# Two cross-attention blocks on one core: GpSimd instead of ScalarE normalises one head in four of the second block

## What is computed

```python
x = layer_norm(hidden_states, ln1_w, ln1_b)
q = (x @ q_w + q_b).reshape(B, LQ, H, HD).transpose(0, 2, 1, 3)
k = (encoder_hidden_states @ k_w + k_b).reshape(B, LK, H, HD).transpose(0, 2, 1, 3)
v = (encoder_hidden_states @ v_w + v_b).reshape(B, LK, H, HD).transpose(0, 2, 1, 3)
scores = jnp.einsum('bhqd,bhkd->bhqk', q, k) * scale
scores = jnp.where(mask, scores, mask_value)
attn = jax.nn.softmax(scores, axis=-1)
out = jnp.einsum('bhqk,bhkd->bhqd', attn, v)
hidden = out.transpose(0, 2, 1, 3).reshape(B, LQ, D) @ cproj_w + cproj_b + residual
```

## Time and profile before

| | us |
|---|---|
| median of three runs | 2257.14 |
| the profiled execution's own time | 2260.57 |
| its span, first to last instruction | 2258.8 |
| TensorE busy in the span | 2161.1 (96%) |
| VectorE busy | 1605.4 (71%) |
| ScalarE busy | 1183.9 (52%) |
| GpSimd busy | 943.8 (42%) |
| second block's attention, logits of step 0 to the last turns | about 1793 to 2090 |

### The profile page before, as it was taken

One profiled execution on the slowest core, in us unless ns is written; L12 is line 12 of the kernel. 1 busy time (PEld: TensorE's weight loads), 2 busy tenths in 40 slices (PEclk: granted clock), 3 DMA queues, 4 the chain that ended last, 5 costly groups with the idle time before them and its releaser, 6 DMA issues.

```text
span 2258.8 us, 36858 instructions
## 1 busy us (share of the span) xinstructions
PE 2161.1 (96%) x12468; PEld 2099.6 (93%) x12468; DVE 1605.4 (71%) x3635; ACT 1183.9 (52%) x2838; POOL 943.8 (42%) x898
## 2 busy tenths in 40 slices
PE   6999999999999999999999999999999899998899
PEld 5999999999999999999999999998899778887899
DVE  6777688777778877777887777777466487788353
ACT  4555465555555555555555555565243376667232
POOL 4314444241444424234342424432788332232597
PEclk9999999999999999999999999999999999998999
DMA  4646455554645555464555546454543667765243
GB/s 136 140 87 142 102 121 101 120 128 83 151 101 113 102 125 122 85 148 105 110 110 116 126 83 151 109 102 83 139 125 103 167 189 199 206 199 160 84 132 108
DMA packets 162454, 283.08 MB, mean 125 GB/s; under 512 B 35424, under 2 KB 92896, under 8 KB 162272
## 3 DMA queue, kind: packets, MB, share of 16 engines
q1 hardware_dynamic: 162272, 280.73, 52.5%
HBM read 237.66 MB, written 29.88 MB: 118 GB/s over the span
## 4 chain that ended last, share of the span: by engine, by line
PE 80%; DVE 6%; DMA 4%; ACT 3%; POOL 3%; issue 2%; SPq 2%; POOLq 0%; DVEq 0%; ACTq 0%
PE bank L838 76%; PE bank L926 3%; POOL mring L759 1%; DMA ctxN_raw<-in_ctx 1%; POOL mring L757 1%; DVE ln_c L1548 1%; DVE hT L1495 1%; SPq L636 1%; DVE lnb L1541 1%; PE bank L1106 1%; ACT prob L1340 1%; DMA k<-k_parts 1%; DVE prob L1662 1%; POOL ln_c L813 1%; DMA y_parts<-qs 0%
## 5 line engine op out<-in xcount | busy, mean ns | idle before, releaser
L838 PE MATMUL bank<-ctxT,kring 128*128 128x362 f32 x3456 | 629.6, 330 | 4.4 <-DVE qs L1495 2.7
L757 POOL TENSOR_SCALAR mring<-stage 128x512 fp32r<-128x512 f32 x325 | 233.3, 718 | 899.2 <-PE bank L838 734.2
L838 PEld LDWEIGHTS bank<-ctxT,kring 128*128 128x128 f32 x3456 | 587.2, 190 | 7.6 <-issue 4.7
L838 PE MATMUL bank<-pT,ctxN 128*128 128x400 f32 (+1 forms) x2304 | 470.0, 351 | 0.6 <-DVE U L1499 0.3
L759 POOL TENSOR_TENSOR mring<-stage,mring 128x512 fp32r<-128x512 f32 x325 | 444.9, 1369 | 27.1
L838 PEld LDWEIGHTS bank<-pT,ctxN 128*128 128x128 f32 (+1 forms) x2304 | 407.1, 188 | 2.4 <-issue 1.2
L838 PE MATMUL bank<-hT,mring 128*128 128x400 f32 x1608 | 320.0, 348 | 13.8 <-DVE hT L1495 10.5
L838 PEld LDWEIGHTS bank<-hT,mring 128*128 128x128 f32 x1608 | 296.1, 190 | 18.3 <-issue 15.0
L838 PE MATMUL bank<-U,mring 128*128 128x400 f32 x1536 | 303.3, 348 | 8.1 <-issue 6.3
L838 PEld LDWEIGHTS bank<-U,mring 128*128 128x128 f32 x1536 | 275.3, 188 | 10.3 <-issue 7.9
L1234 ACT ACTIVATE kT<-bank,cols 128x361 fp32r<-128x361 f32 (+1 forms) x288 | 160.8, 558 | 211.8 <-PE bank L838 211.7
(11 more groups left out here) (103 smaller groups left out, 2942.1 us busy)
## 6 DMA issues: line engine op xcount, KB each, us to landing
ctxT_raw<-in_ctx SPq DMA_DIRECT2D x72, 724.0 KB, 7.5
ctxN_raw<-in_ctx SPq DMA_DIRECT2D x256, 192.0 KB, 3.6
k<-k_parts SPq DMA_DIRECT2D x96, 181.0 KB, 3.7
stage<-in_wk SPq DMA_DIRECT2D x64, 256.0 KB, 4.1
stage<-in_wq SPq DMA_DIRECT2D x64, 256.0 KB, 4.5
stage<-in_wv SPq DMA_DIRECT2D x64, 256.0 KB, 4.0
stage<-in_wo SPq DMA_DIRECT2D x64, 256.0 KB, 2.7
stage<-in_fa SPq DMA_DIRECT2D x64, 256.0 KB, 2.6
```

Source lines behind the costliest of these rows:

```text
L757: nc.gpsimd.tensor_scalar(hi, src, 1.0, 1.0, ALU.mult, ALU.mult).then_inc(S.w_hi, 1)
L838: mm = pe.matmul(dst, parts_l[a], parts_r[b], start=first and k == 0, stop=last and k == len(order) - 1)
```

## The change

ScalarE's `normalise1` and its call are removed. GpSimd gets a `normalise1(s)` for head 4s+1: it waits for the reciprocal and multiplies the row in place with a TENSOR_SCALAR. The turn of this head waits for GpSimd's semaphore `p1_pool` instead of `p1_act`. In GpSimd's list the new entry is due at step s + 0.6 with priority 1. The context split of a batch element, one entry with both halves due at 2.2, becomes two entries, due 2.2 and 3.2.

```diff
-        S.p1_act = sem("p1_act")
+        S.p1_pool = sem("p1_pool")
...
-        def by_act(u):
+        def by_pool(u):
             return u % HG == 1
...
-            def split_context(i):
-
+            def second_context(n):
+
+                b, k = divmod(n, 2)
+                i = 4 * GN + b
                 pool.wait_ge(S.ctxT_in[i % 2], 16 * (i // 2 + 1))
-                for k in range(2):
-                    a = slice(k * HALF_T, (k + 1) * HALF_T)
-                    src, hi = ctxT_raw[:, i % 2, 1, a], ctxT[:, i % 2, 0, a]
-                    nc.gpsimd.tensor_scalar(hi, src, 1.0, 1.0, ALU.mult, ALU.mult).then_inc(S.cT_hi, 1)
-                    pool.wait_ge(S.cT_hi, 2 * i + k + 1)
-                    nc.gpsimd.tensor_tensor(ctxT[:, i % 2, 1, a], src, f32(hi), ALU.subtract).then_inc(S.cT_lo, 1)
-
-            def second_context(b):
-                split_context(4 * GN + b)
+                a = slice(k * HALF_T, (k + 1) * HALF_T)
+                src, hi = ctxT_raw[:, i % 2, 1, a], ctxT[:, i % 2, 0, a]
+                nc.gpsimd.tensor_scalar(hi, src, 1.0, 1.0, ALU.mult, ALU.mult).then_inc(S.cT_hi, 1)
+                pool.wait_ge(S.cT_hi, 2 * i + k + 1)
+                nc.gpsimd.tensor_tensor(ctxT[:, i % 2, 1, a], src, f32(hi), ALU.subtract).then_inc(S.cT_lo, 1)
+
+            def normalise1(s):
+                u = s * HG + 1
+                k = u % PB
+                pool.wait_ge(S.rden1_ready, u + 1)
+                x = prob1[0:LQ, k, 1:LT]
+                nc.gpsimd.tensor_scalar(x, x, rden[0:LQ, k:k + 1], 1.0, ALU.mult, ALU.mult).then_inc(S.p1_pool, 1)
...
-            extra += [(T_ATT1 + 4 * (b - 2) + 2.2, 2, second_context, b) for b in range(2, BATCH)]
+            extra += [(T_ATT1 + 4 * (b - 2) + 2.2 + k, 2, second_context, 2 * b + k)
+                      for b in range(2, BATCH) for k in range(2)]
+            extra += [(T_ATT1 + s + 0.6, 1, normalise1, s) for s in range(NS)]
...
             def turn1(u):
-                if by_act(u):
-                    pe.wait_ge(S.p1_act, u // HG + 1)
+                if by_pool(u):
+                    pe.wait_ge(S.p1_pool, u // HG + 1)
...
-            def normalise1(u):
-                act.wait_ge(S.rden1_ready, u + 1)
-                x, k = prob1[0:LQ, u % PB, 1:LT], u % PB
-                nc.scalar.activation(x, x, ACT.Identity, scale=rden[0:LQ, k:k + 1]).then_inc(S.p1_act, 1)
...
-                    if 0 <= u - 1 < NU1 and by_act(u - 1):
-                        normalise1(u - 1)
```

More of the change, by code:

```diff
@@ L1839, in _ @@
                         inverse1(u - 1)
-                    if 0 <= u - 1 < NU1 and not by_act(u - 1):
+                    if 0 <= u - 1 < NU1 and not by_pool(u - 1):
                         normalise1(u - 1)
```

## The result

The changed kernel took 2304.74 us as the median of four runs (2301.39 to 2307.31) against 2257.44 us for the kernel before (four runs, 2255.45 to 2263.1): ratio 1.021, 95% interval 1.0194 to 1.0226, 47.3 us slower. The forecast was 2313 us with 2288 to 2335. The profiled executions are 2303.11 and 2260.57 us, their spans 2301.3 and 2258.8, 42.5 us apart.

A forecast was written before the change was run, and what follows sets the result against it. Taken as bound by TensorE, busy 96%, its turns in fixed order. Stalls 60.6, given back -10.3, clock +7.9, ScalarE -2 make +56.2 us on the profiled 2260.57; carried over to the median 2257.14, 2313 us, range 2288 to 2335.

The forecast's parts named there:

- six named entries: GpSimd's queue: norm scale (steps 6, 27), tiles and context half (14), norm sum and tiles (20), squares' sum (23), tiles (30).
- The places: Steps 6, 14, 20, 23, 27, 30: GpSimd's release plus 0.55 us minus TensorE's turn, 60.6 us of stalls.
- The instruction: GpSimd's new 100x361 TENSOR_SCALAR, 32 times: 0.50 us each, bounds 0.49 to 0.89.
- The clock: TensorE at half clock after stalls, less two episodes that go with the key waits: +7.9 us, bounds 0 and +12.
- What is given back: Two key waits vanish and part of the last stall is hidden at the end: together -10.3 us.
- two key waits: TensorE's waits for keys, 2.85 and 4.50 us, behind SyncE's wait for the fourth tile's split, would go.
- The end: SyncE's store of step 31's head sums, ready earlier but held by the split: 2.9 us of the last stall hidden.
- port term: GpSimd's normalises and context halves beside VectorE's work at the shared port: 0, within 2 us; blocking rival +16 us, chance 0.07.
- ScalarE's relief: Copies queued behind ScalarE's normalise in the last steps come sooner: -2 us.
- ScalarE was to be 18.6 us less busy: Sign: removing 32 ScalarE instructions of 0.582 us lowers its busy time by 18.6 us.
- GpSimd's wait for the fourth tile of step 14: Sign: GpSimd's wait for fourth tiles, once 24.94 us before, stays as long as before.

The follow-up runs named there:

- the experiment with the earlier load: Changed kernel, but SyncE loads weight tiles by those due in step s instead of s - 1, GpSimd's order unchanged: 2279.07 us, ratio 1.0096.
- spread tiles and ScalarE normalising: Kernel before, ScalarE still normalising, weight tiles due one a step instead of four at once: 2251.42 us, ratio 0.9968.
- the halves together: Changed kernel with normalise due s - 0.1 (step 0 at 0.6), tiles one a step, both context halves in one entry: 2246.79 us, ratio 0.9958.
- earlier places and spread tiles: Changed kernel with normalise due s - 0.1 (step 0 at 0.6) and weight tiles one a step, context halves apart: 2243.01 us, ratio 0.9941.

## Why the prediction was right, point by point

The mechanism held: six stalls behind six named entries. The rise of the profiled execution was forecast as 56.2 us and measured as 42.5, 13.7 too much. That the median came nearer (2304.74 against 2313.3, 8.6 us) is luck: the profiled execution of before lay above its median and that of after below its own, which hides 5 us.

**The places.** The six steps were read off the sorted list, and the six stalls came at them. The only other wait of a turn over 2 us in the changed kernel is one of 2.48 us in step 29, for VectorE. Turn by turn the changed kernel lost 6.8, 15.3, 13.3, 5.2, 7.2 and 11.3 us more than the head before it (differences of the turns' starts between the two traces), 59.0 in all, forecast 7.0, 16.4, 13.2, 4.7, 7.6 and 11.7, 60.6. The release times of the trace of before could be used because what released GpSimd didn't hang on the late turn; the experiment with the earlier load shows the load as the release for the tiles. The one of step 14 came out 1.1 us shorter since the tile landed 3.6 us after its issue (1935.00 to 1938.59) and not 4.6 us.

**The instruction** was priced at 0.50 us from the row of a constant multiply and took 0.57, inside the bounds:

```profile
L789 POOL TENSOR_SCALAR prob<-prob,stat x32: 567/568/575, 1797.3 to 2130.8; 100x361 f32<-100x361 f32 x32
```

**The clock.** After the stalls of steps 6, 14, 20, 23 and 27 the following heads lost another 2.4, 2.3, 2.3, 1.9 and 0 us against the kernel before, 8.9 against 11.3 charged. The windows of the changed kernel behind the longest stall (length, busy and count of PE, PEld, DVE, ACT, POOL, granted clock, DMA share, GB/s) read like the earlier trace rows:

```profile
1943.70:1948.70 5.00, 4.99 (x19) 4.88 (x20) 2.86 (x7) 2.01 (x5) 2.45 (x2) 0.50 0.01 3
1950.50:1955.50 5.00, 5.00 (x30) 4.37 (x29) 3.97 (x15) 3.13 (x9) 0.57 (x1) 1.00 0.12 50
```

At 0.50 (1.2 GHz) 19 matmuls against 30 at 1.00 (2.4 GHz). A stall of 15 us cost no more in clock than the one of 6.6 us. The 0 behind step 27 doesn't mean that the clock stayed up there: it was at 0.56 of full speed on the mean, and a pause of 1.23 us that the kernel before had at this place was gone. The next turn came 3.37 us after this one, against 3.42 us with the pause, so the clock cost some 1.2 us here too. The first row is of the changed kernel, the second of the kernel before:

```profile
2089.00:2092.50 3.50, 3.43 (x14) 3.38 (x15) 1.95 (x6) 1.59 (x4) 0.02 (x1) 0.56 0.00 0
...
2053.99 0.38 PE L1095 MATMUL bank<-k,q 96*100 96x362 f32 x1 [1.23 <-issue]
```

**What is given back** was too small. The two key waits with their stretches of half clock were charged 10.8 us (7.4 and 3.4); the traces show 6.5 between steps 15 and 18 and 6.3 in step 22, 12.8. The end gives back more: the last stalled turn is 49.7 us later than before, the store of step 31's head sums 45.0 (2132.55 against 2087.56), the first matmul of the projection 44.0 (2149.43 against 2105.46), and the end of the span 42.5. That is 7.2 us where 2.9 was charged. The last 1.5 us of it lie behind the projection's first matmul, where the kernels are the same, so they may be chance:

```profile
2132.55 0.33 SPq L626 DMA_DIRECT2D y_parts<-qs  x1
...
2149.43 3.00 PE L845 MATMUL bank<-qT,w 128*128 128x400 f32 x8 [5.75 <-DMA qT<-y_parts]
```

**Not in the sum** were 5.0 us that the changed kernel won back between steps 7 and 10. In the kernel before two low parts of the norm took 2.84 us there, beside a context subtraction:

```profile
1875.86 2.84 DVE L1495 SCALAR_TENSOR_TENSOR hT<-ln_c,cols,hT 128x400 fp32r<-128x400 f32 x2
```

```profile
1875.45 1.74 POOL L781 TENSOR_TENSOR ctxT<-ctxT_raw,ctxT 128x724 fp32r<-128x724 f32 x1
```

In the changed kernel GpSimd's subtraction starts at 1885.15, after them, and they take 1.17 us:

```profile
1882.13 1.17 DVE L1495 SCALAR_TENSOR_TENSOR hT<-ln_c,cols,hT 128x400 fp32r<-128x400 f32 x2
```

In the kernel before the pair took 1.7 us more, and VectorE's normalise behind it 0.8 us more (1.22 us at 1879.26, beside GpSimd's second subtraction, where the median is 0.41). TensorE's next turn waited for the work behind both, and at this turn 2.8 us of the 5.0 were won back:

```profile
1881.00 0.28 PE L1106 MATMUL bank<-ident,prob 100*128 100x100 f32 x1 [2.75 <-DVE pT L1499]
```

L1499 is the low part of the turned probabilities. In the changed kernel TensorE came to this turn without a pause. Behind the wait the kernel before had a stretch of half clock (windows, columns as above), which costs up to 1.7 us and has gone; the next two heads won 1.1 us:

```profile
1881.90:1885.30 3.40, 3.40 (x12) 2.71 (x11) 1.69 (x6) 2.44 (x8) 0.00 (x0) 0.50 0.03 5
```

Such collisions hang on when a load lands: GpSimd had waited for the context in both kernels (16.27 us before, 3.64 after). With spread tiles and ScalarE normalising the same pair took 2.79 us, but TensorE waited only 0.47 us behind it, and that kernel won 2.8 us there. The rest is not separated. The port term of 0, within 2 us, thus held for the new instruction (VectorE is busy 1605.3 us against 1605.4) and not for the old ones around it, whose collision with GpSimd moved to where TensorE waited only 0.27 us (VectorE's normalise of 1885.22 in the changed kernel took 1.90 us). The Trainium skill's rule (SBUF — State Buffer, Who interferes with whom) names this second case as well, a VectorE instruction with two SBUF inputs beside a GpSimd instruction that reads SBUF: by that rule the two exclude each other. The trace of before agrees, with 1.76 us for the longest of its four low parts of this norm (ns, min/median/max) against 0.62. That one began 0.41 us after the subtraction and ended 0.43 us after the subtraction's end:

```profile
L1495 DVE SCALAR_TENSOR_TENSOR hT<-ln_c,cols,hT x4: 624/891/1761, 1867.0 to 1877.5; 128x400 fp32r<-128x400 f32 x4
```

**ScalarE's relief** was charged -2. It can't be seen in the changed kernel beside the stalls. With spread tiles, where nothing stands ahead of the normalise, the move was worth 2.3 us by the ratios with the halves together and 6.1 with them apart, the first within the noise and the second at its edge, so the term is neither confirmed nor refuted.

**Signs that did not come as forecast.** ScalarE was to be 18.6 us less busy and was 12.6 (1171.3 against 1183.9): the count fell by 32, but in the trace its instructions overlap at their ends (the normalise of 1798.51 ran to 1799.09, the next started at 1799.00), and busy time counts an overlap once. GpSimd's wait for the fourth tile of step 14 was to stay as long and fell from 24.94 to 13.39 us, since the first three tiles now stand behind the normalise of step 13; the load's own place against TensorE's turn stayed, and that is what the sum needed.

The sum in one line: stalls 59.0, clock 8.9, key waits -12.8, the end -7.2, steps 7 to 10 -5.0, and small items of together -0.5 (the stretch starts 1.3 us earlier; steps 0 to 5 -0.2; steps 21 to 23 +1.4; steps 25 and 26 -2.3; up to step 27 +0.2; steps 28 to 30 +1.7) make 42.4; the spans differ by 42.5. The medians are 47.3 apart, as the profile of before lies 3.1 us above its median and that of after 1.6 below its own. Forecast were 56.2: the mechanism and its six sizes held, and the terms for what is given back were short by some 11 us (key waits 2.0, the end 4.3, steps 7 to 10 5.0). The stalls were 1.6 and the clock behind them 2.4 us too high, and the -2 for ScalarE doesn't show.

## What to carry to other kernels

In this kernel an instruction that another engine waited for within a step stood, in an in-order queue, behind entries that waited for something of their own, and that made the six stalls. That the engine was free 58% of the time said nothing on this. So when you move such an instruction, list what stands ahead of each copy of the instruction, take the release time of that entry from the trace, and subtract the time at which the consumer wants it. Where work is moved to an engine with slack, look at the long entries in its queue at the same time. Here earlier places and spread tiles turned 47 us of loss into 14 us of gain, of which 5 to 7 come from the tiles without any move.

## What was not expected

Four tiles due at once held two queues, not one: GpSimd waits for the fourth load, and SyncE for the fourth split before it goes on with the keys. Spreading them over four steps is worth 5 to 7 us in the kernel before by itself (0.9968, 0.9954 to 0.9982), with the same work.

GpSimd's TENSOR_SCALAR on 100x361 took 0.57 us with a column of scalars from memory and 0.50 us with constants; both were in place, float32.
